# A graph-attention kernel on one core: the scalar engine's exponential and cast put ahead of the second tile's mask bias

## The chip, the core and the metric

One core of a Trainium2 chip runs the whole kernel. The metric is the device time of one execution in microseconds (us), as a median over runs. The engines are named as in the profile: PE multiplies matrices, DVE is the vector engine, ACT the scalar engine, POOL the GpSimd engine, and SP issues the DMAs.

## The reference

For 4096 nodes with 256 features (h is the row-normalised x with negative values cut to zero, m is masked_x) the reference computes, cut to what matters:

```
lQ = m @ Wlq ; lK = h @ Wlk ; lV = h @ Wlv + blv
local_scores = where(adj, lQ @ lK.T * scale, -1e9)        # 4096 x 4096
max_score = max(rowmax(local_scores), global_scores, es)
le = exp(local_scores - max_score)
denom = sum(le) + ge + ee
res = le / denom @ lV + ge / denom * gV + ee / denom * eV
out = x + maximum(res, m)
```

## The kernel before

Both large products are made in split precision: a value is a high half and a low half in float16, and three products of halves replace one in float32.

**Tiling.** Query rows go in 16 row blocks n of 256 rows, that is two tiles (t = 0, 1) of 128 rows. Keys go in 4 groups g of 1024. A **period** p = 4n + g makes the masked scores of one row block against one key group: 64 periods. A **unit** u = 2p + t is one tile of it, 128 x 1024. Below, "step" is p modulo 4. The first 12 periods (`PC = 12`) make their scores in the plain way; the periods 12 to 63 use the Strassen (Winograd) form, in which seven products p1 to p7 of 512 columns stand for eight.

**PE in a Strassen period** runs, in an order written out by hand: p1(p), p7(p-1), p5(p), p6(p), p4(p-1), p2(p), p3(p), and between them the 16 slices of the second large product, `p_times_v` (rows L995, L997, L999), for units of period p-6.

**DVE in a Strassen period** takes the products out of PSUM into `s32`, adding the mask bias (`out11`, `out12`, `out21`, `out22`, line L1320), and adds shared products into the bias tile (`add11` L1351, `add12` L1357, `add22` L1363). `add22(p)` needs the second tile's bias and p5(p), and p3(p) waits for it. `out22(p-1)` frees what p4(p-1) waits for. At step 0 DVE also makes the row maximum of the finished row block (`row_max`: `mloc` L1370, `mrow` L1372, `mtop` L1374, `negm` L1376). At step 1, between `add11(p)` and `out22(p-1)`, it makes the scales of a later row block's queries (`q_rows` and `q_row_scales`, lines L1214 to L1311; L1226 makes `rtrue`).

**ACT in a period** runs `mask_bias(u)` (line L734: turns 128 x 1024 adjacency bytes into a bias tile, in a ring of three), and for the units of period p-5 the exponential `exp_unit(u)` (L747) and the cast of its result to the high half, `p_high(u)` (L763). The first exponential of a row block, at step 1, waits for `negm`. `p_high(u)` also waits until the DMA transpose of unit u-2 has read its buffer. Per period there are two mask biases: that of the second tile, 2p+1, waits for `out11` and `out12` of period p-1; that of the next period's first tile, 2p+2, waits for `out21` and `out22` of period p-1.

**POOL** makes the low half of each unit, `p_low(u)` (L581), as soon as `p_high(u)` is done; at step 0 it also makes `finish` (L591). **SP** then issues the DMA transpose of the unit (L348) for PE's second product, and the loads of adjacency tiles. Each engine works in the order of its program and waits on semaphores.

After period 63 the last units are drained: the row maximum of row block 15, then eight units (120 to 127) through ACT, POOL, SP's transposes and PE.

Of the kernel before, what the change touches and what calls it, by code (L numbers as in the profile page):

```python
# [24 lines left out]
def build(nc, x, adj, mxT, mx, WlqT, WlkT, Wlv, blv, WgqT, WgkT, Wgv, bgv, Wes, Wev, bev, out):  # L25
# [6 lines left out]
    NPER = NP * NG  # L32
    PC = 12
# [17 lines left out]
    with ExitStack() as ctx:  # L51
# [188 lines left out]
        def ring(count, size):  # L240
            return 16 * (count // size + 1)
# [392 lines left out]
        def _(act):  # L634
# [39 lines left out]
            def v_high(n):  # L674
                act.wait_ge(s_vp, n + 1)
                nc.scalar.activation(v_rows[:, 2 * n:2 * n + 2, 0:D],
                                     v_bank(n).rearrange("p (k d) -> p k d", k=2), ACT.Copy,
                                     scale=V_SCALE / (H_SCALE * W_SCALE)).then_inc(s_vhi, 1)

            def q_scale(n):  # L680
                act.wait_ge(s_cq, n + 1)
                act.wait_ge(s_gsc, n + 1)
                if n >= 2:
                    act.wait_ge(s_qlo, n - 1)
                for t, at in ((1, A21), (0, A11)):
                    rows = f32q[:, at:at + 2] if n == 1 else ps_q[:, t, 0:D].rearrange("p (c d) -> p c d", c=DC)
                    scale = cqs[:, t:t + 1] if n >= QH else cq[:, n % 2, t:t + 1]
                    nc.scalar.activation(f32q[:, at:at + 2], rows, ACT.Copy, scale=scale).then_inc(s_qf, 1)

            def weights_high():  # L690
                act.wait_ge(s_nscale, 1)
                act.wait_ge(s_gev, 5)
                nc.scalar.activation(m_hl[:, 0], mge[:, :, :], ACT.Copy, scale=nscale[:, 0:1]).then_inc(s_mwhi, 1)

            def wev_high():
                act.wait_ge(s_mwlo, 1)
                act.wait_ge(s_q, QH)
                nc.scalar.activation(wev_hl[:, 0], wev_sb[:, :, :], ACT.Copy, scale=nscale[:, 1:2]).then_inc(s_wvhi, 1)

            def mx_high(n):  # L700
                act.wait_ge(s_mscale, n - QH + 1)
                act.wait_ge(s_qT[(n - 1) % 2], ring(n - 1, 2))
                for t in range(2):
                    nc.scalar.activation(mx_rows[:, t], mx_rows[:, t], ACT.Copy, scale=mscale[:, t:t + 1]).then_inc(s_ms, 1)
                act.wait_ge(s_ms, 2 * (n - QH + 1))
                nc.scalar.activation(mx_hl[:, :, 0], mx_rows, ACT.Copy).then_inc(s_mhi, 1)

            def q_high(n):
                if n >= 1:
                    act.wait_ge(s_qT[(n - 1) % 2], ring(n - 1, 2))  # L710
                if NG * n >= PC:
                    act.wait_ge(s_qs, 4 * (n - PC // NG + 1))
                    nc.scalar.activation(q_hl[:, 0], f32q[:, 1:8], ACT.Copy).then_inc(s_qhi, 1)
                else:
                    act.wait_ge(s_qf, 2 * n + 3)
                    nc.scalar.activation(q4[:, 0], f32q[:, 0:4], ACT.Copy).then_inc(s_qhi, 1)
# [3 lines left out]
            def mask_bias(u):  # L720
                p, t = u // 2, u % 2
                n = p // NG
                if t == 0:
                    act.wait_ge(s_adj[p % 2], ring(p, 2))
                    act.wait_ge(s_big, 2 * n + 2)
                if u >= NBI:
                    v = u - NBI
                    if v % 2 == 0:
                        act.wait_ge(s_o11, v // 2 + 1)
                        act.wait_ge(s_o12, v // 2 + 1)  # L730
                    else:
                        act.wait_ge(s_o21, v // 2 + 1)
                        act.wait_ge(s_o22, v // 2 + 1)
                nc.scalar.activation(bias[:, u % NBI].rearrange("p b k -> p (b k)"), adj8[:, p % 2, t], ACT.Identity,  # L734
                                     bias=big[:, n % 2, 1, t:t + 1], scale=big[:, n % 2, 0, t:t + 1]
                                     ).then_inc(s_bias, 1)

            def exp_unit(u):
                p, t = u // 2, u % 2
                n, g = p // NG, p % NG  # L740
                if u % (2 * NG) == 0:
                    act.wait_ge(s_negm, n + 1)
                    if n == 0:
                        act.wait_ge(s_hlo, rows_done(NB - 1))
                    else:
                        act.wait_ge(s_w, n - 1)
                nc.scalar.activation(s32[:, p % NS, t], s32[:, p % NS, t], ACT.Exp, bias=negm[:, n % 2, t:t + 1],  # L747
                                     scale=invc[:, n % 4, t:t + 1], accum_out=psums[:, n % 2, t, g:g + 1]
                                     ).then_inc(s_exp, 1)

            def side_exp(n):
                for t in range(2):
                    nc.scalar.activation(mass[:, n % 2, t, 1:3], gs_es[:, n % 4, t], ACT.Exp,
                                         bias=negm[:, n % 2, t:t + 1]).then_inc(s_ge, 1)

            def p_high(u):
                p, t = u // 2, u % 2
                act.wait_ge(s_exp, u + 1)
                if u >= LAST + NBI:
                    act.wait_ge(*turned(u - NBI - 2))  # L760
                elif 2 <= u < LAST:
                    act.wait_ge(*turned(u - 2))
                nc.scalar.activation(p_rows(u)[:, 0], s32[:, p % NS, t], ACT.Copy).then_inc(s_phi, 1)  # L763
# [33 lines left out]
            for n in V_AT[NB]:  # L797
                v_high(n)
            for p in range(4, NPER + LAG_E):
                if p < NPER:  # L800
                    mask_bias(2 * p + 1)
                n = (p + 3) // NG
                u = 2 * (p - LAG_E)
                live = 0 <= u < 2 * NPER
                if p == 4:
                    for k in V_AT[9][0:2]:
                        v_high(k)
                    exp_unit(0)
                    p_high(0)
                    side_exp(0)  # L810
                    for k in V_AT[9][2:6]:
                        v_high(k)
                if live and u:
                    exp_unit(u)
                    p_high(u)
                    if u % (2 * NG) == 0:
                        side_exp((p - LAG_E) // NG)
                if p % NG == 2 and 2 <= n < NP:
                    q_high(n)
                if p == 7:  # L820
                    weights_high()
                if p == 9:
                    wev_high()
                if live:
                    exp_unit(u + 1)
                    p_high(u + 1)
                if p == 4:
                    for k in V_AT[9][6:8]:
                        v_high(k)
                if p % NG == 3 and QH <= (p + 5) // NG < NP:  # L830
                    mx_high((p + 5) // NG)
                if p + 1 < NPER:
                    mask_bias(2 * p + 2)
                if p % NG == 1 and 2 <= n < NP:
                    q_scale(n)
# [872 lines left out]
```

## Time and profile before

| | |
|---|---|
| median of 3 runs | 747.29 us (746.12 to 749.49) |
| profiled execution, its time | 745.91 us |
| its span | 744.1 us |
| PE busy | 721.6 us |
| DVE, ACT, POOL busy | 561.1, 532.8, 443.8 us |
| granted PE clock, mean | 0.995 of full speed |

The span runs from the first to the last instruction; the execution's own time is 1.8 us longer. Busy time is the time in which an engine has an instruction in work. All rows below are of this one profiled execution, and times in them are counted from the start of its span.

### The profile page before, as it was taken

The numbers are of one execution on the slowest core, as the hardware profiler recorded it, in microseconds if no ns is written. First come the engines' busy times: TensorE is split into PE (matmuls) and PEld (weight loads), VectorE is DVE, ScalarE is ACT, GpSimd is POOL, SyncE is SP. The second block draws the span as 40 slices with busy tenths as digits, with TensorE's granted clock in tenths as the row PEclk, the third lists the DMA queues.
The fourth block names the chain that finished last, engine by engine and source line by source line (L and its number), as shares of the span: only waits on it lengthen the run. The fifth ranks groups of instructions, "written<-read, shape, count | busy, mean of one in ns | idle before, by whom it ended". The sixth has DMA issues, their size and how long they took to land. (4 is left out here: it accounts for less than half of the span.)

```text
span 744.1 us, 14652 instructions
## 1 busy us (share of the span) xinstructions
PE 721.6 (97%) x5212; PEld 509.9 (69%) x5212; DVE 561.1 (75%) x1379; ACT 532.8 (72%) x701; POOL 443.8 (60%) x307
## 2 busy tenths in 40 slices
PE   7699999999999999999999999999999999999987
PEld 6366566666767777676767777676677777676776
DVE  5776677899677878778686778778686878677685
ACT  5783788666877777867877776868767776857690
POOL 2459579869566554655556554665556554653493
PEclk9899999999999999999999999999999999999999
DMA  7975277868898698897978898897978897968798
GB/s 205 234 190 102 55 159 151 185 127 172 182 176 174 138 212 152 160 178 160 194 151 175 142 209 157 168 169 166 185 151 178 137 217 150 172 139 181 131 190 151
DMA packets 366154, 123.20 MB, mean 166 GB/s; under 512 B 326272, under 2 KB 366080, under 8 KB 366080
## 3 DMA queue, kind: packets, MB, share of 16 engines
q1 hardware_dynamic: 366080, 122.26, 81.9%
q8 instruction: 41, 0.67, 0.4%
q14 instruction: 33, 0.27, 0.1%
HBM read 36.57 MB, written 4.19 MB: 55 GB/s over the span
## 5 line engine op out<-in xcount | busy, mean ns | idle before, releaser
L581 POOL TENSOR_TENSOR p_base<-s,p_base 128x1024 f16<-128x1024 f32 x108 | 232.3, 2154 | 229.5 <-ACT p_base L763 229.4
L995 PE MATMUL ps_u<-v_rows,pT_base 128*128 128x256 f16 x968 | 263.9, 273 | 3.2 <-DMA pT_base<-p_base 2.8
L997 PE MATMUL ps_u<-v_rows,pT_base 128*128 128x256 f16 x968 | 263.9, 273 | 0.0
L999 PE MATMUL ps_u<-v_rows,pT_base 128*128 128x256 f16 x968 | 263.9, 273 | 0.0
L734 ACT ACTIVATE bias<-adj,big 128x1024 f32<-128x1024 uint8 x128 | 157.8, 1237 | 118.3 <-DVE bmax L1320 109.2
L763 ACT ACTIVATE p_base<-s 128x1024 f16<-128x1024 f32 x122 | 129.0, 1057 | 42.5 <-DMA pT_base<-p_base 39.5
L747 ACT ACTIVATE s<-s,negm,invc 128x1024 f32<-128x1024 f32 x128 | 157.0, 1226 | 0.0
L995 PEld LDWEIGHTS ps_u<-v_rows,pT_base 128*128 128x128 f16 x968 | 94.7, 98 | 56.0 <-DMA pT_base<-p_base 3.3
L997 PEld LDWEIGHTS ps_u<-v_rows,pT_base 128*128 128x128 f16 x968 | 94.7, 98 | 52.1
L1320 DVE CUSTOM_DVE_ANT_0 s<-ps_x,bias 128x512 f32<-128x512 f32 x128 | 88.1, 689 | 46.2 <-PE ps_x L898 41.7
L999 PEld LDWEIGHTS ps_u<-v_rows,pT_base 128*128 128x128 f16 x968 | 94.7, 98 | 10.9
L896 PE MATMUL ps_x<-hT,qT 128*128 128x512 f16 x152 | 58.1, 382 | 2.1 <-DVE bmax L1320 2.1
L898 PE MATMUL ps_x<-hT,qT 128*128 128x512 f16 x152 | 58.1, 382 | 0.0
L897 PE MATMUL ps_x<-hT,qT 128*128 128x512 f16 x152 | 58.1, 382 | 0.0
L1320 DVE CUSTOM_DVE_ANT_0 s<-ps_w,bias 128x512 f32<-128x512 f32 x64 | 43.9, 685 | 13.4 <-PE ps_w L898 10.6
L1320 DVE CUSTOM_DVE_ANT_0 s<-ps_v,bias 128x512 f32<-128x512 f32 x64 | 43.8, 685 | 12.0 <-PE ps_v L898 11.5
L1351 DVE TENSOR_TENSOR bias<-ps_x,bias 128x512 f32<-128x512 f32 x52 | 35.9, 690 | 21.6 <-PE ps_x L898 17.5
L1363 DVE TENSOR_TENSOR bias<-ps_v,bias 128x512 f32<-128x512 f32 x52 | 35.8, 688 | 14.2 <-PE ps_v L898 14.1
L1357 DVE TENSOR_TENSOR bias<-ps_x,bias 128x512 f32<-128x512 f32 x52 | 35.8, 689 | 11.5 <-PE ps_x L898 11.4
L896 PE MATMUL ps_x<-hW,qT 128*128 128x512 f16 x104 | 39.4, 379 | 1.5 <-DVE bmax L1320 1.5
L897 PE MATMUL ps_x<-hW,qT 128*128 128x512 f16 x104 | 39.4, 379 | 0.0
L898 PE MATMUL ps_x<-hW,qT 128*128 128x512 f16 x104 | 39.4, 379 | 0.0
(217 smaller groups left out, 1272.1 us busy)
## 6 DMA issues: line engine op xcount, KB each, us to landing
adj<-adj SPq DMA_DIRECT2D x64, 256.0 KB, 3.5
s<-x SPq DMA_DIRECT2D x7, 512.0 KB, 5.0
f32q<-mx SPq DMA_DIRECT2D x14, 256.0 KB, 3.9
xm<-x SPq DMA_DIRECT2D x14, 256.0 KB, 3.5
xm<-mx SPq DMA_DIRECT2D x14, 256.0 KB, 4.0
out<-t_sb SPq DMA_DIRECT2D x14, 256.0 KB, 3.3
pT_base<-p_base SPq DMA_TRANSPOSE x120, 4.5
mxT_f<-mxT SPq DMA_DIRECT2D x4, 256.0 KB, 5.1
```

The lines of the kernel that those rows point to most:

```text
L581: nc.gpsimd.tensor_tensor(p_rows(u)[:, 1], s32[:, p % NS, u % 2], p_rows(u)[:, 0], ALU.subtract).then_inc(s_plo, 1)
L734: nc.scalar.activation(bias[:, u % NBI].rearrange("p b k -> p (b k)"), adj8[:, p % 2, t], ACT.Identity, bias=big[:, n % 2, 1, t:t + 1], sc ...
L747: nc.scalar.activation(s32[:, p % NS, t], s32[:, p % NS, t], ACT.Exp, bias=negm[:, n % 2, t:t + 1], scale=invc[:, n % 4, t:t + 1], accum_o ...
L763: nc.scalar.activation(p_rows(u)[:, 0], s32[:, p % NS, t], ACT.Copy).then_inc(s_phi, 1)
L896: nc.tensor.matmul(bank, q_form(n, f, 1), keys(0), start=start, stop=False, skip_group_check=True)
L897: nc.tensor.matmul(bank, q_form(n, f, 0), keys(1), start=False, stop=False, skip_group_check=True)
L898: return nc.tensor.matmul(bank, q_form(n, f, 0), keys(0), start=False, stop=stop, skip_group_check=True)
L995: nc.tensor.matmul(acc, turn[:, 0, j], v_rows[:, kc, 0:D], start=opens, stop=False, skip_group_check=True)
L997: nc.tensor.matmul(acc, turn[:, 0, j], v_rows[:, kc, D:2 * D], start=False, stop=False, skip_group_check=True)
L999: done = nc.tensor.matmul(acc, turn[:, 1, j], v_rows[:, kc, 0:D], start=False, stop=end, skip_group_check=True)
L1320: nc.vector.tensor_tensor_reduce(out=s32[:, p % NS, t, b * BLOCK:(b + 1) * BLOCK], in0=bank, in1=bias[:, u % NBI, b], scale=1.0, scalar=-3 ...
L1351: nc.vector.tensor_tensor(at, ps_x[:, p % 2], at, ALU.add).then_inc(s_a11, 1)
```

## The change

In the periods 12 to 63 the mask bias of the second tile, `mask_bias(2p+1)`, no longer stands first on ACT. It comes after the first exponential and cast of the period (and after the small `side_exp` where there is one). The first 12 periods keep their order. Nothing is added or removed, and no wait of any instruction is changed.

```
             for p in range(4, NPER + LAG_E):
-                if p < NPER:
-                    mask_bias(2 * p + 1)
                 n = (p + 3) // NG
                 u = 2 * (p - LAG_E)
                 live = 0 <= u < 2 * NPER
+                if p < PC:
+                    mask_bias(2 * p + 1)
...
                     if u % (2 * NG) == 0:
                         side_exp((p - LAG_E) // NG)
+                if PC <= p < NPER:
+                    mask_bias(2 * p + 1)
                 if p % NG == 2 and 2 <= n < NP:
                     q_high(n)
```

On ACT, at the turn from period 36 (step 0) to period 37 (step 1), the order before is this. `bias<-adj` is a mask bias, `s,psums<-s` an exponential, `p_base<-s` a cast; the bias that waits for `s_o12,s_o11` is that of the second tile.

```order
L734 ACTIVATE bias<-adj,big 128x1024 [waits s_o12,s_o11]
L747 ACTIVATE s,psums<-s,negm,invc 128x1024
L763 ACTIVATE p_base<-s 128x1024 [waits s_pT0,s_exp]
L747 ACTIVATE s,psums<-s,negm,invc 128x1024
L763 ACTIVATE p_base<-s 128x1024 [waits s_pT1,s_exp]
L734 ACTIVATE bias<-adj,big 128x1024 [waits s_o21,s_o22,s_big,s_adj1]
L734 ACTIVATE bias<-adj,big 128x1024 [waits s_o12,s_o11]
L747 ACTIVATE s,psums<-s,negm,invc 128x1024 [waits s_w,s_negm]
L763 ACTIVATE p_base<-s 128x1024 [waits s_pT2,s_exp]
L753 ACTIVATE mass<-gs_es,negm 128x2 x2
```

And with the change, at the same place:

```order
L747 ACTIVATE s,psums<-s,negm,invc 128x1024
L763 ACTIVATE p_base<-s 128x1024 [waits s_pT0,s_exp]
L734 ACTIVATE bias<-adj,big 128x1024 [waits s_o12,s_o11]
L747 ACTIVATE s,psums<-s,negm,invc 128x1024
L763 ACTIVATE p_base<-s 128x1024 [waits s_pT1,s_exp]
L734 ACTIVATE bias<-adj,big 128x1024 [waits s_o21,s_o22,s_big,s_adj1]
L747 ACTIVATE s,psums<-s,negm,invc 128x1024 [waits s_w,s_negm]
L763 ACTIVATE p_base<-s 128x1024 [waits s_pT2,s_exp]
L753 ACTIVATE mass<-gs_es,negm 128x2 x2
L734 ACTIVATE bias<-adj,big 128x1024 [waits s_o12,s_o11]
```

Both biases of the second tile moved down, behind the first exponential and cast of their period; at step 1 the exponential that waits for `negm` now has no wait for `s_o12,s_o11` ahead of it.

The second place is ACT in the last Strassen period, 63, before:

```order
L734 ACTIVATE bias<-adj,big 128x1024 [waits s_o21,s_o22,s_big,s_adj1]
L734 ACTIVATE bias<-adj,big 128x1024 [waits s_o12,s_o11]
L747 ACTIVATE s,psums<-s,negm,invc 128x1024
L763 ACTIVATE p_base<-s 128x1024 [waits s_pT0,s_exp]
L747 ACTIVATE s,psums<-s,negm,invc 128x1024
```

And with the change:

```order
L734 ACTIVATE bias<-adj,big 128x1024 [waits s_o21,s_o22,s_big,s_adj1]
L747 ACTIVATE s,psums<-s,negm,invc 128x1024
L763 ACTIVATE p_base<-s 128x1024 [waits s_pT0,s_exp]
L734 ACTIVATE bias<-adj,big 128x1024 [waits s_o12,s_o11]
L747 ACTIVATE s,psums<-s,negm,invc 128x1024
```

Here one mask bias, the last of all, moved behind the exponential and cast of unit 116; the one ahead of them (unit 126) stayed.

## Rows read from the trace of the kernel before

**Rows 1.** Page, part 1: busy us, share of the span, instructions
```profile
PE 721.6 (97%) x5212; PEld 509.9 (69%) x5212; DVE 561.1 (75%) x1379; ACT 532.8 (72%) x701; POOL 443.8 (60%) x307
```

**Rows 2.** Windows: length, then busy us of PE, PEld, DVE, ACT, POOL; PEclk
```profile
165.00:675.00 510.00, 508.50 (x3641) 357.05 (x3639) 388.88 (x976) 380.10 (x485) 294.36 (x192) 1.00 0.85 169
675.00:744.00 69.00, 62.39 (x515) 49.76 (x512) 48.81 (x86) 38.19 (x50) 39.18 (x20) 0.99 0.89 165
```

**Rows 3.** Waits of the whole span: who waited for whom, total us, times, longest
```profile
POOL p_base L581 <- ACT p_base L763: 229.4, 85, 5.9
ACT bias L734 <- DVE bmax L1320: 109.2, 73, 4.5
ACT p_base L763 <- DMA pT_base<-p_base: 39.5, 27, 4.8
```

**Rows 4.** Timeline of ACT, periods 36 and 37: start, us, instruction, [idle before]
```profile
408.70 1.24 ACT L734 ACTIVATE bias<-adj,big 128x1024 f32<-128x1024 uint8 x1 [0.87 <-DVE bmax L1320]
...
413.51 1.06 ACT L763 ACTIVATE p_base<-s 128x1024 f16<-128x1024 f32 x1
...
419.68 1.24 ACT L734 ACTIVATE bias<-adj,big 128x1024 f32<-128x1024 uint8 x1 [3.23 <-DVE bmax L1320]
420.82 1.23 ACT L747 ACTIVATE s<-s,negm,invc 128x1024 f32<-128x1024 f32 x1
...
422.17 1.06 ACT L763 ACTIVATE p_base<-s 128x1024 f16<-128x1024 f32 x1
```

**Rows 5.** Timeline of POOL, the same periods
```profile
412.33 4.44 POOL L581 TENSOR_TENSOR p_base<-s,p_base 128x1024 f16<-128x1024 f32 x2 [3.32 <-ACT p_base L763]
416.74 1.26 POOL L591 TENSOR_TENSOR t_sb<-t_sb,xm 128x512 f32<-128x512 f32 x1
423.31 2.13 POOL L581 TENSOR_TENSOR p_base<-s,p_base 128x1024 f16<-128x1024 f32 x1 [5.31 <-ACT p_base L763]
```

**Rows 6.** Timeline of DVE, the same periods
```profile
411.40 0.69 DVE L1363 TENSOR_TENSOR bias<-ps_v,bias 128x512 f32<-128x512 f32 x1 [0.60 <-PE ps_v L898]
...
415.43 1.36 DVE L1372 TENSOR_TENSOR mrow<-mloc,invc 128x2 f32<-128x2 f32 x1
416.82 1.19 DVE L1374 TENSOR_TENSOR mtop<-mrow,ges 128x2 f32<-128x2 f32 x1
418.05 0.17 DVE L1376 TENSOR_SCALAR negm<-mtop 128x2 f32<-128x2 f32 x1
...
421.23 0.16 DVE L1226 TENSOR_TENSOR rtrue<-rmax,mu 128x2 f32<-128x2 f32 x1
...
422.65 0.69 DVE L1320 CUSTOM_DVE_ANT_0 s<-ps_x,bias 128x512 f32<-128x512 f32 x1
```

**Rows 7.** Timeline of PE: first matmul of p3(36), then of p4(36)
```profile
416.42 0.38 PE L896 MATMUL ps_v<-hT,qT 128*128 128x512 f16 x1
...
424.60 0.38 PE L896 MATMUL ps_x<-hW,qT 128*128 128x512 f16 x1
```

**Rows 8.** Timeline of DVE, periods 28 and 29
```profile
335.19 0.17 DVE L1376 TENSOR_SCALAR negm<-mtop 128x2 f32<-128x2 f32 x1
...
337.95 0.16 DVE L1226 TENSOR_TENSOR rtrue<-rmax,mu 128x2 f32<-128x2 f32 x1
...
339.71 0.69 DVE L1320 CUSTOM_DVE_ANT_0 s<-ps_x,bias 128x512 f32<-128x512 f32 x1
```

**Rows 9.** Timeline of PE: first matmul of p4(28)
```profile
341.12 0.38 PE L896 MATMUL ps_x<-hW,qT 128*128 128x512 f16 x1
```

**Rows 10.** Timeline of ACT at the end: cast of unit 118, exponential of unit 120
```profile
702.78 1.06 ACT L763 ACTIVATE p_base<-s 128x1024 f16<-128x1024 f32 x1 [4.83 <-DMA pT_base<-p_base]
...
706.06 1.23 ACT L747 ACTIVATE s<-s,negm,invc 128x1024 f32<-128x1024 f32 x1
```

**Rows 11.** Timeline of DVE at the end: the last row maximum
```profile
703.72 0.17 DVE L1376 TENSOR_SCALAR negm<-mtop 128x2 f32<-128x2 f32 x1
```

**Rows 12.** Timeline of PE at the end
```profile
710.99 0.28 PE L995 MATMUL ps_u<-v_rows,pT_base 128*128 128x256 f16 x1 [2.83 <-DMA pT_base<-p_base]
```

More of the change, by code:

```diff
@@ L799, in _ @@
             for p in range(4, NPER + LAG_E):
-                if p < NPER:
-                    mask_bias(2 * p + 1)
                 n = (p + 3) // NG
@@ L804, in _ @@
                 live = 0 <= u < 2 * NPER
+                if p < PC:
+                    mask_bias(2 * p + 1)
                 if p == 4:
@@ L817, in _ @@
                         side_exp((p - LAG_E) // NG)
+                if PC <= p < NPER:
+                    mask_bias(2 * p + 1)
                 if p % NG == 2 and 2 <= n < NP:
```

## The prediction

> **What bounds the kernel now.** I read the page's busy times first: PE is in work for 97% of the span [rows 1]. The question is then where its idle time lies, and the windows answer it: in the 510 us of the Strassen periods PE is idle for 1.5 us, at full clock, while in the last 69 us it is idle for 6.6 us [rows 2]. So the middle is bound by PE's own work and can get no faster by another engine's order; it can only get slower, where some engine begins to come too late for PE. Only the end has time to give back. Next the waits: POOL's low half waits 229 us for ACT's cast, ACT's mask bias waits 109 us for DVE, and the cast waits 39.5 us for a transpose [rows 3]. These are long but off the path: PE waits for none of them in the middle. The change trades among exactly these waits, so what matters is not their sum but the spare time of each thing that PE needs.
>
> **The change, part by part.** Nothing is added: two instructions of 1.24 us and 2.3 us trade places in 52 periods. Four effects follow.
>
> *The exponential and cast start earlier.* At step 0 (period 36) ACT is free 0.87 us before its bias at 408.70, so at 407.83 [rows 4]. From there the spacing of the rows holds: 1.35 us from exponential to cast (420.82 to 422.17), 0.96 us of cast, 1.14 us from a bias to what follows it (419.68 to 420.82) [rows 4]. The first cast then starts at 409.18, and the bias at 410.14. In the middle this gains nothing, because PE never waits for these units.
>
> *The second tile's bias ends later.* In period 36 it would end at 410.14 + 1.24 = 411.38, where it now ends at 409.94. `add22` takes it at 411.40 [rows 4, 6], a time set by PE, so the bias is just in time. I made this subtraction for all 52 periods; where the cast must also wait for its transpose the bias comes later, and in 16 periods `add22` would start late, by at most about 2.2 us. What stands behind it: p3(36) begins at 416.42, while `add22` ends at 412.09 [rows 6, 7], which leaves 4.3 us. The other DVE operations behind `add22` have idle gaps ahead of them, which swallow the rest in the same period. Price: nothing on PE. If that cover were gone, each microsecond late would be one on PE.
>
> *POOL's low half moves onto DVE's small operations at step 1.* This is the term that I did not find in the diff but in the rows. DVE's `mrow` and `mtop` should take 0.16 us each, like `rtrue`, which is as small; they take 1.36 and 1.19 us, and they end at 416.79 and 418.01, together with POOL's low half at 416.77 and its `finish` at 418.00 [rows 5, 6]: while POOL runs an operation, such a DVE operation waits for its end. The 128x512 operations that read PSUM keep their 0.69 us beside POOL, so they do not wait. The Trainium skill has this in "SBUF — State Buffer", section "Who interferes with whom": the two engines share a pair of ports as an exclusive lock, and a tensor_tensor with both inputs in SBUF, or a tensor_scalar, waits for a GpSimd instruction's whole length. By that rule the change is a risk, and the rows above agree with it.
> At step 1 POOL is idle before 423.31, and DVE's chain of small operations runs undisturbed from 421.23 to 422.65, where `out22` starts [rows 5, 6]. POOL's start is tied to ACT's cast (422.17 + 1.14 = 423.31), which was held back by the mask bias at 419.68 [rows 4]. With the bias behind it, the exponential can start 0.07 us after `negm`, which ends at 418.22 [rows 6]. So POOL starts at 418.22 + 0.07 + 1.35 + 1.14 = 420.78, holds 2.14 us to 422.92, and `rtrue` starts then instead of at 421.23: 1.69 us late, and the chain and `out22` with it. `out22` now ends at 423.34, 1.26 us before p4(36) at 424.60 [rows 6, 7]. PE would wait 1.69 - 1.26 = 0.43 us.
> In period 29 the same sum is 335.36 + 2.56 + 2.14 = 340.06 against `rtrue` at 337.95, so 2.11 us late, with 341.12 - 340.40 = 0.72 us to spare [rows 8, 9]: PE waits 1.39 us. Eleven periods have this chain (17, 21, ... 57; in 13 POOL comes behind other work of its own and does not move). Eight are like 37 (spare 1.25 or 1.26, lateness 1.5 to 1.7), 29 has the thinnest spare, and 25 and 41 lie between (spare 1.10 and 0.92, lateness 2.1). Their sum is 8 x 0.39 + 1.39 + 1.00 + 1.16 = 6.7 us.
> But `negm` itself comes earlier. It was late by POOL's second low half at step 0, whose cast moves from 413.51 to 407.83 + 1.35 + 0.96 + 1.14 + 1.35 = 412.63, so 0.88 us earlier [rows 4]; POOL's `finish` follows, `mtop` is released 0.85 us earlier, and POOL's low half at step 1 ends 0.85 us earlier too. Lateness then falls by 0.85: the eight fit in their spare time, and 0.54 + 0.15 + 0.31 = 1.0 us is left. In about half of the blocks this gain will not come, because the second cast at step 0, or the first at step 1, waits for its transpose anyway (those 39.5 us [rows 3]). I take 0.4 us of gain for all: 8 x 0.03 + 0.99 + 0.60 + 0.76 = 2.6 us. Bounds: nothing below (if the small operations slip in before POOL), 6.7 above.
>
> *The end.* PE's longest wait there is 2.83 us at 710.99, for a transpose [rows 12]. It comes from ACT: the cast of unit 118 waited until 702.78, and so the exponential of unit 120 starts only at 706.06, although `negm` was there at 703.89 [rows 10, 11]. From there a dense chain runs (ACT, POOL, transposes) to the last product. One mask bias fewer ahead of unit 116 brings this chain forward by 1.14 us [rows 4]. It can gain at most 706.06 - 703.89 = 2.2 us, and nothing if the cast of unit 119 is held by a transpose that waits for PE. I take 1.1 us.
>
> **The sum.** 745.91 + 2.6 - 1.1 = 747.4 us for an execution like the profiled one, whose time was 1.4 us below the median of the runs; against the median it is 747.29 + 1.5 = 748.8 us.
>
> **The rivals.**
> *Only the end counts.* The collision at step 1 stays within the spare time, since the eight ordinary blocks need only 0.43 us of luck each. For it: DVE can be first at any of its ten small operations, and then POOL waits. Against it: three blocks have less spare time. Time: 747.3 - 1.1 = 746.2 us.
> *The collision costs in full.* `negm` does not come earlier, since the second cast at step 0 is bound by its transpose. For it: the 39.5 us in 27 waits [rows 3]. Time: 747.3 + 6.7 - 1.1 = 752.9 us, which is slower. It decides when the lateness of `out22` passes 1.26 us, and costs over 0.5% when the eleven blocks lose 4.9 us together.
> *The bias comes too late.* A cast that waits for its transpose now holds up the mask bias, and `add22` passes its 4.3 us. Against it: the latest that I find is 2.2 us, and the longest such wait in the Strassen periods would have to double. If it stalled PE by 1 us in the 13 periods of step 3: 747.3 + 13 - 1.1 = 759 us.
> *A real gain.* PE's idle time after 165 us is 1.5 + 6.6 us, a part of it behind its last product. A gain above 0.5% (3.7 us) would need half of it, 743.5 us.
>
> **How the numbers follow.** A measurement of this kernel can tell about 0.5%, 3.7 us, from no change. Chances: my forecast 0.45, only the end 0.27, the full collision 0.18, the late bias 0.04, the real gain 0.06. The forecast reaches past +3.7 us in one case of ten (0.05), the full collision in nearly all (0.17), the late bias always: slower 0.26. Faster: 0.07. Same: 0.67. The range goes from the end's full gain (747.3 - 2.2, 745.1) to the full collision, 752.9. The forecast's own range is 746.5 to 751.
>
> **What would show it.** In the changed profile: ACT's wait of the bias for DVE shrinks well below 109 us, and POOL's wait for the cast falls little; the biases of step 0 end just before `add22`. At step 1 one of `rtrue` to `ges` takes 0.5 to 2.1 us, ending with POOL's low half, and PE shows waits for DVE before p4, most of all near 341 and 466 us; the sum of these waits is the first term. At the end the exponential of unit 120 starts nearer to `negm`, and PE's 2.83 us shrinks. I am wrong if DVE's small operations at step 1 keep their 0.16 us, if PE waits elsewhere (before p3), or if the last chain does not move.

## The result, and the profile after

| | before | after |
|---|---|---|
| median of 14 runs each, same comparison | 746.12 us (743.51 to 749.55) | 748.34 us (745.48 to 751.87) |
| ratio after / before | | 1.0039, 95% interval 1.0021 to 1.0057 |
| profiled execution, its time; its span | 745.91; 744.1 | 748.33; 746.5 |

The kernel is 0.4% slower, 2.9 us by the ratio and 2.2 us by the two medians: a loss that 14 runs tell from zero, but smaller than 0.5%. The forecast was 1.5 us slower, 748.8 us.

The page's busy times after, which answer to [rows 1]:

```profile
PE 722.6 (97%) x5212; PEld 509.7 (68%) x5212; DVE 576.7 (77%) x1379; ACT 530.4 (71%) x701; POOL 442.8 (59%) x307
```

DVE has the same 1379 instructions and is busy for 15.6 us more. An operation of DVE that waits inside itself for POOL counts as busy, so this is the first sign of the collision: only the order of ACT was changed, and DVE's work grew.

The windows after, with the columns of [rows 2]:

```profile
165.00:675.00 510.00, 504.92 (x3604) 353.10 (x3603) 406.09 (x972) 375.93 (x483) 291.84 (x191) 1.00 0.85 168
```

In the Strassen periods PE was idle for 1.5 us before, in one wait before p4 in period 13; now it is idle for 5.1 us, that wait included, at the same full clock, and DVE is busy for 17 us more. The loss lies in the middle.

The waits of the whole span after (who waited for whom, total us, times, longest), the first three as in [rows 3]:

```profile
POOL p_base L581 <- ACT p_base L763: 212.8, 98, 5.9
ACT bias L734 <- DVE bmax L1322: 88.1, 44, 4.5
ACT p_base L763 <- DMA pT_base<-p_base: 48.3, 41, 4.7
...
DVE bias L1365 <- ACT bias L734: 19.2, 15, 2.0
```

ACT's wait for DVE and POOL's for ACT moved as the prediction said; the cast's wait for its transpose grew by 9 us, which it did not say. The last row is the late mask bias: `add22` waits for it in 15 places, at most 2.0 us (forecast: 16 places, at most 2.2 us).

Which products PE then waited for is in its timeline (start, us, instruction, idle before). Three of its five waits for DVE in the periods after 15, before p4 in period 17, before p3(26) and before p4 in period 41:

```profile
215.13 0.39 PE L898 MATMUL ps_x<-hW,qT 128*128 128x512 f16 x1 [0.57 <-DVE bmax L1322]
...
312.67 0.39 PE L898 MATMUL ps_v<-hT,qT 128*128 128x512 f16 x1 [0.76 <-DVE bias L1365]
...
467.92 0.39 PE L898 MATMUL ps_x<-hW,qT 128*128 128x512 f16 x1 [0.82 <-DVE bmax L1322]
```

To size the loss I took the start of every product of both traces and looked where their difference grows. It starts at -1.10 us, since the first Strassen product began at 156.31 before and at 155.21 after; that shift stands already at 96 us, long ahead of the first moved instruction. It then grows in six steps and falls once:

| where | PE waits for | growth, us |
|---|---|---|
| p4, period 17 | `out22` | 0.74 |
| p3(26) | `add22` | 0.94 |
| p4, period 41 | `out22` | 1.01 |
| p3(46) | `add22` | 0.81 |
| p3(50) | `add22` | 0.93 |
| p4, period 53 | `out22` | 0.15 |
| the end | | -1.08 |

The growth at a wait is a little more than the idle time shown; that of period 53 is too small to be shown as a wait. The sum is 4.58 - 1.08 = 3.5 us; less 1.10 of the earlier start, with which the change has nothing to do, it is the 2.4 us between the spans. For one profiled execution of a kernel I therefore count below from the first Strassen product to the end of the span: 744.1 - 156.31 = 587.8 us before, 746.5 - 155.21 = 591.3 us after.

**Step 1.** The dearest block is the one of period 41. DVE's timeline after:

```profile
463.83 2.06 DVE L1228 TENSOR_TENSOR rtrue<-rmax,mu 128x2 f32<-128x2 f32 x1
465.93 0.17 DVE L1232 TENSOR_SCALAR rclamp<-rtrue 128x2 f32<-128x2 f32 x1
...
467.16 0.69 DVE L1322 CUSTOM_DVE_ANT_0 s<-ps_x,bias 128x512 f32<-128x512 f32 x1
```

And POOL's:

```profile
463.75 2.13 POOL L581 TENSOR_TENSOR p_base<-s,p_base 128x1024 f16<-128x1024 f32 x1 [2.76 <-ACT p_base L763]
```

POOL starts 0.08 us ahead of `rtrue`, which then takes 2.06 us in place of the 0.16 us of [rows 6] and ends with POOL's operation, at 465.89 against 465.88. `out22` ends at 467.85, and PE starts p4 at 467.92. `rtrue` is slowed in all eleven blocks, to 0.69 to 0.88 us in seven of them, to 1.18 and 1.49 us in two, and to 2.06 and 2.08 us in periods 41 and 17. The seven fit into the spare time.

Which blocks fit goes by `negm`. Counted from p3 of the same step 0, it ends 0.8 to 1.6 us earlier than before in the seven, 0.5 us earlier in the block of period 57, but only 0.06 and 0.03 us earlier in those of 41 and 53, and 0.4 us later in that of 17. In periods 40 and 52 ACT's second cast waited 2.82 and 1.97 us for its transpose, at most 1.7 us in the other blocks, and that took the gain away. The cast of period 40:

```profile
456.50 1.06 ACT L763 ACTIVATE p_base<-s 128x1024 f16<-128x1024 f32 x1 [2.82 <-DMA pT_base<-p_base]
```

**Step 2.** Here is what I had not forecast. At step 2 DVE makes the side rows of the finished row block (`side_rows`, L1414 and L1417, four operations), and then `add22(p)`. Period 26 before, on DVE and POOL:

```profile
306.60 0.48 DVE L1412 SCALAR_TENSOR_TENSOR r_base<-gv_b,w,blv_b 128x256 f32<-128x256 f32 x1
307.12 0.48 DVE L1415 SCALAR_TENSOR_TENSOR r_base<-bev_b,w,r_base 128x256 f32<-128x256 f32 x1
307.52 0.68 DVE L1363 TENSOR_TENSOR bias<-ps_v,bias 128x512 f32<-128x512 f32 x1
...
308.24 2.14 POOL L581 TENSOR_TENSOR p_base<-s,p_base 128x1024 f16<-128x1024 f32 x1 [2.99 <-ACT p_base L763]
```

And after:

```profile
305.24 2.28 DVE L1417 SCALAR_TENSOR_TENSOR r_base<-bev_b,w,r_base 128x256 f32<-128x256 f32 x1
...
308.06 1.49 DVE L1414 SCALAR_TENSOR_TENSOR r_base<-gv_b,w,blv_b 128x256 f32<-128x256 f32 x1
309.58 2.43 DVE L1417 SCALAR_TENSOR_TENSOR r_base<-bev_b,w,r_base 128x256 f32<-128x256 f32 x1
311.94 0.68 DVE L1365 TENSOR_TENSOR bias<-ps_v,bias 128x512 f32<-128x512 f32 x1
...
305.11 2.13 POOL L581 TENSOR_TENSOR p_base<-s,p_base 128x1024 f16<-128x1024 f32 x1 [0.48 <-ACT p_base L763]
307.20 2.07 POOL L568 TENSOR_TENSOR q_hl<-f32q,q_hl 128x896 f16<-128x896 f32 x1
309.61 2.13 POOL L581 TENSOR_TENSOR p_base<-s,p_base 128x1024 f16<-128x1024 f32 x1 [0.34 <-ACT p_base L763]
```

Before, POOL's train of three operations began at 308.24, just when `add22` had ended (308.20). Now ACT makes the cast before the second tile's bias, the train begins at 305.11, and three of the four side rows take 1.49 to 2.43 us in place of 0.48. `add22` ends at 312.62, and PE starts p3 at 312.67. Before, 3.9 us lay between these two (308.20 to 312.09). No wait of DVE for ACT stands ahead of `add22` here: the bias was there in time, DVE was not. Periods 46 and 50 are alike: three side rows slowed, and `add22` ends 0.05 us before p3. In the other step-2 periods from 18 to 58 two side rows are slowed, and `add22` still ends 0.7 to 1.1 us before p3. Five of those eight (22, 30, 34, 38, 58) differ from the three only by POOL's second low half. In the three it started 0.09 us ahead of the fourth side row or at most 0.02 us behind it; ACT's cast ahead of it had waited 0.13 to 0.24 us for its transpose. In the five that cast waited 0.43 to 1.6 us, the low half started 0.2 to 1.4 us behind the side row, and the side row kept its 0.48 us. Period 34 is the closest:

```profile
394.00 0.48 DVE L1417 SCALAR_TENSOR_TENSOR r_base<-bev_b,w,r_base 128x256 f32<-128x256 f32 x1
394.21 2.27 POOL L581 TENSOR_TENSOR p_base<-s,p_base 128x1024 f16<-128x1024 f32 x1 [0.52 <-ACT p_base L763]
```

The Trainium skill, "SBUF — State Buffer", section "Who interferes with whom", says that a DVE instruction with two SBUF inputs contends with a GpSimd instruction that reads SBUF; the rows of period 26 agree, 2.28 and 2.43 us beside POOL against 0.48 us alone.

**The end.** The exponential of unit 120 and PE's longest wait, which answer to [rows 10] and [rows 12]:

```profile
707.91 1.06 ACT L763 ACTIVATE p_base<-s 128x1024 f16<-128x1024 f32 x1 [4.67 <-DMA pT_base<-p_base]
708.88 1.23 ACT L747 ACTIVATE s<-s,negm,invc 128x1024 f32<-128x1024 f32 x1
...
711.78 0.28 PE L997 MATMUL ps_u<-v_rows,pT_base 128*128 128x256 f16 x1 [0.20 <-DMA pT_base<-p_base]
```

PE's 2.83 us shrank to 0.20 us. PE now comes 3.5 us later to this part (p3(63) starts at 700.97, at 697.47 before) and finds its data nearly ready. It wins 2.7 us there and loses 1.6 us again further on, most of it in a new wait of 0.99 us for a transpose at 723.86; what is left is the 1.08 us of the table. The chain of ACT moved less than forecast: from p3(63) to the exponential of unit 120 it is 7.91 us, 8.59 before. The cast shown here is that of unit 119, which now waited 4.67 us for its transpose; with the last bias alone moved it waited 2.18 us, so this is probably what took a part of the gain, which no run isolates.

### The profile page after: what moved, and what is told of

It reads as the page before. It is cut to its first block and busy times, and to the rows that moved or that the text cites. A ratio compares the mean times of both kernels' runs of the same rounds, so it can differ in the third digit from the quotient of the medians.

```text
span 746.5 us, 14652 instructions
## 1 busy us (share of the span) xinstructions
PE 722.6 (97%) x5212; PEld 509.7 (68%) x5212; DVE 576.7 (77%) x1379; ACT 530.4 (71%) x701; POOL 442.8 (59%) x307
## 5 line engine op out<-in xcount | busy, mean ns | idle before, releaser
L1353 DVE TENSOR_TENSOR bias<-ps_x,bias 128x512 f32<-128x512 f32 x52 | 35.8, 689 | 23.7 <-PE ps_x L900 22.5
L1417 DVE SCALAR_TENSOR_TENSOR r_base<-bev_b,w,r_base 128x256 f32<-128x256 f32 x30 | 42.0, 1400 | 1.1
L898 PE MATMUL ps_x<-hW,qT 128*128 128x512 f16 x104 | 39.5, 379 | 2.9 <-DVE bmax L1322 2.9
L899 PE MATMUL ps_x<-hW,qT 128*128 128x512 f16 x104 | 39.4, 379 | 0.0
```

The source lines that it names most:

```text
L898: nc.tensor.matmul(bank, q_form(n, f, 1), keys(0), start=start, stop=False, skip_group_check=True)
L899: nc.tensor.matmul(bank, q_form(n, f, 0), keys(1), start=False, stop=False, skip_group_check=True)
L1417: nc.vector.scalar_tensor_tensor(r12[:, t], bev_b[:, :], w3[:, t, 1:2], r12[:, t], ALU.mult, ALU.add).then_inc(s_r, 1)
```

## The experiments

All ratios are to the kernel before, run in the same comparison; its medians there were 745.91, 746.32 and 746.04 us, of 23 or 24 runs. Times "from the first Strassen product" are those of the profiled execution, as above, against 587.8 us before. Every kernel with DVE's old order also has the wait before p4 in period 13, 1.4 to 1.5 us; it is left out where waits are counted.

### One step put back

The moved bias stands in `if PC <= p < NPER`. The other condition is complementary, so each of these kernels moves a part of the 52 biases.

```
 e1_step2_back:   moved only where p % NG != 2
 e2_step1_back:   moved only where p % NG != 1
 e3_steps12_back: moved only where p % NG in (0, 3)
 e4_last_only:    moved only where p == NPER - 1
```

**Step 2 back.**

> The changed order at steps 0, 1 and 3 of a row block's four periods; at step 2 the second tile's bias stands first again, as in the kernel before. Collision theory (POOL's low half holds back small or two-input DVE operations in SBUF): at step 2 POOL starts late again, DVE's four side-row operations take 0.48 us each, and the three waits of PE before p3 (2.2 us in waits, 2.7 us of lag) are gone; the step 1 lag of about 1.9 us stays. Ratio to before about 1.001 (0 to +0.2%). Rival, the late mask bias: the p3 waits come from the bias itself; it would give the same at step 2, but then add22 must have been seen waiting for ACT there, and steps 0 and 3, where the bias is late too, should show p3 waits as well.

Measured: 747.98 us (12 runs), ratio 1.0022 (1.0005 to 1.0040); 588.4 us from the first Strassen product, +0.6. No wait before any p3; three waits before p4, 0.57, 0.20 and 0.76 us. So in the trace the step-2 loss goes when step 2 goes back, and the step-1 loss stays; the ratio alone does not tell this kernel from after, since the intervals overlap.

**Step 1 back.**

> The changed order at steps 0, 2 and 3; at step 1 the old order. Collision theory: DVE's rtrue at step 1 takes 0.16 us in all eleven blocks and PE has no wait before p4 (1.9 us of lag gone); the p3 waits of step 2 (2.7 us of lag) stay. Ratio about 1.002. Rival (lag is from elsewhere): p4 waits stay.

Measured: 749.15 us (6 runs), ratio 1.0051 (1.0031 to 1.0071); 591.0 us, +3.1. The opposite of what I expected: six waits before p4, of 0.53 to 0.59 us, each a growth of 0.7 us, and none before p3. The collision at step 1 comes although ACT's order at step 1 is the old one. Step 2 collides here too, but with one side row fewer: in period 26 POOL's train starts at 308.08, two side rows take 1.75 and 2.00 us, and `add22` ends at 313.42, 1.1 us before p3.

**Steps 1 and 2 back.**

> The changed order at steps 0 and 3 only. Collision theory: no PE wait in the Strassen periods beyond the one of 1.5 us near 172 us, and the end keeps its gain of 1.1 us: ratio 0.9985 (within 0.2% of before). Rival (late mask bias): add22 is late at steps 0 and 3 by up to 2 us as in the full change, so PE would wait before p3 there and the ratio would stay above 1.002.

Measured: 749.02 us (7 runs), ratio 1.0041 (1.0018 to 1.0064); 590.5 us, +2.7. Five waits before p4, 0.53 to 0.59 us. Also a miss, and the one that corrected my theory. Period 29 of this kernel, on three engines:

```profile
340.67 2.13 POOL L581 TENSOR_TENSOR p_base<-s,p_base 128x1024 f16<-128x1024 f32 x1 [5.31 <-ACT p_base L763]
340.75 2.15 DVE L1255 TENSOR_SCALAR big<-cq 128x2 f32<-128x2 f32 x2
342.88 0.68 DVE L1322 CUSTOM_DVE_ANT_0 s<-ps_x,bias 128x512 f32<-128x512 f32 x1
...
343.62 0.39 PE L898 MATMUL ps_x<-hW,qT 128*128 128x512 f16 x1 [0.54 <-DVE bmax L1322]
```

POOL hits `big`, next to the last of DVE's small operations, which takes 2.15 us in place of 0.24. Before, POOL's low half at step 1 came after the whole chain (423.31 against 422.65 [rows 5, 6]), by 0.66 us there. Through the new order at step 0 `negm` comes 0.5 to 1.6 us earlier in eight of the eleven blocks, counted from p3 of step 0 (1.6 us in that of period 29), and with it, at step 1, the exponential, the cast and POOL. In five of them that is enough to fall on the end of the chain. The new order at step 1 brings POOL still earlier, onto the beginning of the chain, where only the rest of POOL's operation counts.

**The last period only.**

> The changed order in period 63 alone. If the last bias ahead of unit 116 is what brought the end forward: from p3(63) to the end of the span about 1.1 us shorter than before (before: 744.1 - 697.5 = 46.6 us), ratio 0.9985. If instead the earlier work of the periods 60 to 62 did it, no gain and 1.000.

Measured: 745.52 us (12 runs), ratio 0.9999 (0.9985 to 1.0013); 586.2 us, -1.6. No wait in the Strassen periods, and at the end PE waits 0.40 us. The chain at the end moves as forecast, for a single moved bias: from p3(63) to the exponential of unit 120 it takes 7.5 us in place of 8.6. The trace is 1.6 us shorter; the medians do not resolve it.

**Step 3 only.** `p % NG == 3`.

> The changed order at step 3 alone, period 63 among them. With the orders of steps 1 and 2 put back PE still waited before p4, where negm came 0.8 us earlier through step 0. If step 0 did that, here the row maximum takes as long as before, PE has no wait before p4, and the ratio is 0.998 to 0.999, the gain of the end. If step 3 did it, the ratio is near 1.004.

Measured: 746.79 us (12 runs), ratio 0.9994 (0.9974 to 1.0013); 586.4 us, -1.4. No wait before p4, and `negm` comes at most 0.2 us earlier in any block. So of steps 0 and 3, step 0 is what brings `negm`, and POOL at step 1, too early.

### POOL kept off DVE's chain

The new order everywhere, and POOL's low half waits at step 1 until `q_rows` is done (`s_ges`), at step 2 until the side rows are (`s_r`):

```
+                if PC < p < NPER and p % NG == 1 and (p + 3) // NG < NP:
+                    pool.wait_ge(s_ges, (p + 3) // NG + 1)
+                if PC < p < NPER and p % NG == 2:
+                    pool.wait_ge(s_r, 4 * ((p - 9) // NG) + 4)
                 if live:
                     p_low(u)
```

> The changed order of ACT everywhere, and one more wait on POOL: at step 1 the first low half waits until DVE has finished its chain of query scales, at step 2 until DVE has finished the side rows. The mask bias is as late as in the full change. Collision theory: rtrue to ges and the side rows take their 0.16 and 0.48 us again, PE waits neither before p4 nor before p3, and the end keeps its gain: ratio 0.998 to 0.999. Rival, the late mask bias: PE's waits before p3 stay (over 2 us of lag), ratio above 1.002.

Measured: 744.81 us (12 runs), ratio 0.9984 (0.9965 to 1.0003); 586.0 us, -1.8. The profiled execution is the slowest of the 12, 749.70 us, since its first Strassen product starts only at 161.86 us; from there on it is shorter than before. Its page and one of its waits:

```profile
PE 726.0 (97%) x5212; PEld 512.3 (69%) x5212; DVE 537.7 (72%) x1379; ACT 529.3 (71%) x701; POOL 440.3 (59%) x307
```

```profile
DVE bias L1369 <- ACT bias L738: 14.5, 11, 2.1
```

DVE is busy for 537.7 us, 39 us less than after and 23 us less than before, with the same instructions. In the Strassen periods PE waits for DVE nowhere else than in period 13. `add22` still waits for the late bias, 11 times and up to 2.1 us: that wait costs nothing. This run decides between the two theories: with POOL held and the bias as late as ever, the loss is gone. At step 1 in the period that answers to 41, DVE and POOL now stand like this:

```profile
468.81 0.16 DVE L1232 TENSOR_TENSOR rtrue<-rmax,mu 128x2 f32<-128x2 f32 x1
...
470.01 0.24 DVE L1259 TENSOR_SCALAR big<-cq 128x2 f32<-128x2 f32 x2
...
470.39 4.28 POOL L581 TENSOR_TENSOR p_base<-s,p_base 128x1024 f16<-128x1024 f32 x2 [4.42 <-DVE ges L1317]
```

POOL starts 1.58 us behind `rtrue`, where it was 0.08 us ahead of it, and nobody on the path needs that time.

**POOL held, only the last bias moved.**

```
-                if PC <= p < NPER:
+                if p < NPER and (p == NPER - 1):
                     mask_bias(2 * p + 1)
```

> ACT's order of before, but the change in period 63 alone, and POOL held at steps 1 and 2 as in the held run. Both gains that were seen are of the end, and they are the same one, so this should not beat either: PE waits nowhere in the Strassen periods, from the first Strassen product to the end 586 us, ratio 0.998 to 0.999. If holding POOL had a gain of its own, it would be clearly under 0.998.

Measured: 744.68 us (12 runs), ratio 0.9982 (0.9961 to 1.0003); 586.1 us, -1.7. The same as with all 52 biases moved. The new order is worth nothing in the middle, with or without the collision; what it can bring is the end.

**POOL held at step 1 only, order of steps 0 and 3.** The third experiment, with the first of the two waits.

> The changed order at steps 0 and 3 (without the hold: ratio 1.0041, five waits before p4), and POOL held at step 1 alone. If the earlier negm only brought POOL onto the last query scales, the waits before p4 are gone: from the first Strassen product to the end 586 to 586.5 us instead of 590.5, ratio 0.998 to 0.999. If step 0's order slows PE in another way, it stays near 1.004.

Measured: 745.63 us (12 runs), ratio 0.9993 (0.9971 to 1.0015); 585.7 us, -2.1; no wait before p4. It confirms what I read in the third experiment: the collision at step 1 was its whole loss.

### The bias made later still

The bias of the second tile behind both exponentials and casts, POOL held:

```
-                if PC <= p < NPER:
-                    mask_bias(2 * p + 1)
...
                 if live:
                     exp_unit(u + 1)
                     p_high(u + 1)
+                if PC <= p < NPER:
+                    mask_bias(2 * p + 1)
```

> The price of a late bias by itself: the second tile's bias behind both exponentials and casts of its period, with POOL held so that there are no collisions. The bias moves another 2.3 us or more, and in many periods the second cast also waits for its transpose. Late-bias rival, at last in its range: add22 comes 3 to 5 us late, more than its 4.3 us of spare time in some periods, and DVE's later operations with it; ratio 1.005 to 1.03. If the ratio stays at 0.999, add22 has far more room than I worked out.

Measured: 770.38 us (6 runs), ratio 1.0328 (1.0294 to 1.0361); 610.3 us, +22.5. Two rows of its waits:

```profile
DVE bias L1369 <- ACT bias L738: 196.5, 52, 6.7
```

```profile
PE ps_v L902 <- DVE bias L1369: 14.8, 13, 4.0
```

`add22` waits in all 52 periods, and where that uses up its cover of 4 us, PE waits before p3, 13 times and up to 4.0 us; five more waits for DVE, up to 1.1 us, stand before other products. So the rival of the late bias has a real price, just above the top of what I had expected; the change simply doesn't reach it: 2.0 us late at most.

### DVE's own order

I tried the other side as well: `out22` ahead of `q_rows`, and `out22` and `add22` ahead of the side rows, with the new order of ACT and, as control, with the old one.

```
+                    if wino(old):
+                        out22(old)
                     if project:
                         q_rows(m)
-                    if step == 2 and ended:
-                        side_rows(done, 0)
-                    if wino(old):
-                        out22(old)
-                    if step == 2 and ended:
-                        side_rows(done, 1)
                     if p < NPER:
                         add22(p)
+                    if step == 2 and ended:
+                        side_rows(done, 0)
+                        side_rows(done, 1)
```

> The changed order of ACT, and DVE's out22 ahead of the query scales at step 1, out22 and add22 ahead of the side rows at step 2. The collisions stay (rtrue is slowed in most blocks), but the operations that PE needs stand before them. Collision theory: no wait before p4 at step 1 or p3 at step 2, ratio 0.998 to 1.000. If the lag has another cause, the ratio stays near 1.004.

> Control: the same order of DVE with ACT's order of before. Nothing was late there, so the median stays: ratio 1.000 (0.998 to 1.002).

Measured: with the new order of ACT 772.20 us (6 runs), ratio 1.0338 (1.0307 to 1.0370); with the old one 756.40 us (6 runs), ratio 1.0151 (1.0119 to 1.0184). Both miss: the control alone is 1.5% slower, so the first says little for or against the collision at step 1, although its trace has no wait before p4 at step 1 and none before p3 at step 2. PE waits before p1 of step 3, up to 0.76 us in the control after nearly every row block, and 0.7 to 3.8 us with ACT's new order. Both also wait once 2.7 us before p3 in period 13, where the wait before p4 is gone. The control's rows in period 26, DVE, POOL, then PE's p1 of period 27:

```profile
312.24 2.36 DVE L1412 SCALAR_TENSOR_TENSOR r_base<-gv_b,w,blv_b 128x256 f32<-128x256 f32 x1
314.64 1.99 DVE L1415 SCALAR_TENSOR_TENSOR r_base<-bev_b,w,r_base 128x256 f32<-128x256 f32 x1
...
317.15 0.67 DVE L1320 CUSTOM_DVE_ANT_0 s<-ps_x,bias 128x512 f32<-128x512 f32 x1
...
312.19 2.13 POOL L581 TENSOR_TENSOR p_base<-s,p_base 128x1024 f16<-128x1024 f32 x1 [1.99 <-ACT p_base L763]
314.28 2.06 POOL L568 TENSOR_TENSOR q_hl<-f32q,q_hl 128x896 f16<-128x896 f32 x1
...
317.89 0.39 PE L896 MATMUL ps_x<-hT,qT 128*128 128x512 f16 x1 [0.68 <-DVE bmax L1320]
```

By moving the side rows behind `add22` I put them under POOL's train even with ACT's old order. The extraction behind them comes at 317.15, too late for PE at step 3. The old place of the side rows had kept them clear of POOL.

## Why the prediction was right and where it was not

**What bounds the kernel: right.** The middle could only lose, and lost; only the end gave back. Moving one bias (-1.6 us in its trace) and moving all with POOL held (-1.8 us) come out alike.

**The second tile's bias ends later, at no price: right.** 15 waits of at most 2.0 us, forecast 16 of at most 2.2. The held kernel keeps these waits and loses nothing, and the kernel with a still later bias shows from where they cost.

**POOL's low half moves onto DVE's small operations at step 1: right in kind, 1.9 us against 2.6.** The operations of `q_rows` take up to 2.08 us in place of 0.16, and end with POOL's operation. The term was mis-sized block by block. I took 0.4 us of relief from the earlier `negm` for every block. In seven blocks it was 0.8 to 1.6 us; they are late by 0.5 to 0.7 us and fit. Period 29, the thinnest by my sum (0.99), is one of them and costs nothing. In periods 41 and 53 the relief did not come, because the second cast at step 0 waited for its transpose. I had named that condition, but for half of the blocks. Period 41 has nearly the forecast cost without relief (growth 1.01; 1.16 without it, 0.76 with it), period 53 has 0.15, and period 17, where `negm` came later, costs 0.74 where I had 0.03. That the sum came near is luck: its parts did not.

**"In the middle this gains nothing": the step that failed.** I asked only what an earlier exponential and cast could gain, and answered nothing. I did not ask on what POOL's earlier low half would fall at the other steps. At step 2 it falls on the side rows; three blocks lose 2.7 us. That is as large as the whole loss that I had forecast for the middle, and it makes up for the too large term of step 1 and more. By my own signs I was wrong here: I had written that PE would wait before p4 near 341 and 466 us and not before p3. It waited at 468, not near 341, and three times before p3. The middle lost 4.6 us where I had 2.6. Of these, 1.9 us are the collision that I forecast and 2.7 us are not. That the forecast of +1.5 us lies near the measured +2.2 us by medians and +2.9 us by the ratio is thus partly luck.

**"But `negm` itself comes earlier": half right.** I counted it as a relief alone. The runs with step 1 in its old order show that by itself it is a cause: the chain of `rtrue` to `ges` stood before only 0.66 us ahead of POOL in period 37, and a `negm` that came 0.5 to 1.6 us earlier was enough for five or six waits of 0.53 to 0.59 us. The parts of the change do not add up: each of them alone puts POOL somewhere else on the chain.

**The end: right, and the close number partly luck.** 1.1 us forecast, 1.08 us in the trace, 1.6 us with the last bias alone. With the last bias alone the exponential of unit 120 came 1.1 us sooner, which is the mechanism as forecast. With all biases moved it came only 0.7 us sooner, probably since the cast of unit 119 was held by its transpose, the condition that I had named.

**The rivals.** *Only the end counts* fell by the waits in the middle. *The collision in full* fell, as eight of eleven blocks fit into their spare time; its condition, a second cast at step 0 bound by its transpose, took `negm`'s gain away in the blocks of 41 and 53 alone. *The bias too late* fell by the held kernel. *A real gain* did not come: the best versions, the two with POOL held, are at 0.9984 and 0.9982 with intervals to 1.0003, so no version here is clearly faster than before.

**Left open.** Why ACT's casts wait for their transposes longer in some periods than in others; this decides by tenths of a microsecond which blocks lose. Also why `negm` came later in the block of period 17. The difference between the ratio of after (+2.9 us) and its trace (+2.4 us in span) is within the spread of the runs.

## What to carry to other kernels

When an engine is made faster off the path, ask for every step, not only for the one that is changed, on which operations of DVE the next POOL operation will now fall. The sign in a profile is an operation of 0.16 us that ends together with POOL's, or one of 0.48 us that ends 0.3 us after it; a margin of less than a microsecond between POOL's start and such a chain is a dependency that no semaphore states. If order matters there, write it down as a wait of the engine that has time, and keep it although the time barely changes: with it, moving one bias and moving all 52 took the same time. It does not make every order free: the bias behind both exponentials and casts cost 24 us even so.

## What the runs showed of the hardware

- How much of DVE's busy time was waiting for POOL: two waits of POOL took 39 us from it against after (576.7 to 537.7 us), with no instruction less. Against before it is 23 us, but that is the hold and the new order together: with ACT's order of before, but for the last bias, the hold left 557.5 of 561.1 us.
- Not only the smallest operations wait for POOL. A `scalar_tensor_tensor` of 128x256 with its tensors in SBUF took 1.49 to 2.43 us in place of 0.48, and a pair of `tensor_scalar` of 128x2 took 2.15 us in place of 0.24. The 128x512 extractions from PSUM took 0.65 to 0.69 us in all these kernels. And a `scalar_tensor_tensor` of the same 128x256 with one of its two tensors in PSUM kept its time, beside POOL too: the second of these rows of the kernel after (shortest, median and longest time in ns), against the first with both in SBUF.

```profile
L1417 DVE SCALAR_TENSOR_TENSOR r_base<-bev_b,w,r_base x30: 483/1625/2431, 145.2 to 713.9; 128x256 f32<-128x256 f32 x30
L1438 DVE SCALAR_TENSOR_TENSOR r_base<-ps_q,wes,r_base x24: 472/477/481, 279.6 to 719.7; 128x256 f32<-128x256 f32 x24
```

- The one that comes second waits, POOL too. A side row that started 0.06 us ahead of POOL's low half (221.35 against 221.41 in the kernel after) kept its 0.48 us, and POOL's took 2.41 us in place of 2.13. At a lead of 0.01 or 0.02 us it was the side row that waited.
- The first Strassen product of the profiled executions starts between 155.2 and 161.9 us, although nothing ahead of it differs in its work. Between before and after most of the difference of 1.1 us comes at 62.7 us, where PE waited 1.45 us for a transpose before and 0.54 us after. Whether this is also the 6 us between the fastest and the slowest run of one kernel no run here shows; the late start of the held kernel's profiled execution, its slowest, fits.
